# First loads of a UNet-like convolution kernel: image 0 cut into 6, 13 and 13 rows, the middle piece issued by ScalarE, and an 8-byte read of each row of the first weights

## The reference, cut to what matters

```python
def _gn(v, G=32, eps=1e-05):
    g = v.reshape(B_, G, C_ // G, H_, W_)
    m = jnp.mean(g, axis=(2, 3, 4), keepdims=True)
    s = jnp.var(g, axis=(2, 3, 4), keepdims=True)
    return ((g - m) / jnp.sqrt(s + eps)).reshape(v.shape)
...
    x = basic_block(x, e0b0c1, e0b0c2)       # 3x3 convs at 64x64
    x = basic_block(x, e0b1c1, e0b1c2)
    f0 = x
    x = basic_block(x, e1b0c1, e1b0c2, stride=2, ds=e1b0ds)   # 32x32
    x = basic_block(x, e1b1c1, e1b1c2)
    f1 = x
    x = basic_block(x, e2b0c1, e2b0c2, stride=2, ds=e2b0ds)   # 16x16
    x = basic_block(x, e2b1c1, e2b1c2)
    x = (relu(deconv2(x, dec0w) * BN_S) + f1) * BN_S
    x = (relu(deconv2(x, dec1w) * BN_S) + f0) * BN_S
...
    x = x + _L0_conv_ref(_gn(x), ...)
```

## Time and profile before

| | us |
|---|---|
| median of three timed runs | 92.99 |
| the profiled execution | 93.48 |
| its span, first to last instruction | 91.3 |
| PE busy | 83.4 (91% of the span) |
| DVE busy | 63.1 (69%) |
| ACT busy | 44.8 (49%) |
| POOL busy | 28.0 (31%) |

### The profile page before, as it was taken

The page is one execution under the profiler, slowest core; times in us unless marked ns, Lnnn a source line. Parts: engine busy times, 40 slices in busy tenths (PEclk is TensorE's granted clock), DMA queues, the critical chain, the costliest instruction groups (busy, mean ns, idle before and its releaser), DMA issues.

```text
span 91.3 us, 1542 instructions
## 1 busy us (share of the span) xinstructions
PE 83.4 (91%) x537; PEld 74.4 (81%) x537; DVE 63.1 (69%) x181; ACT 44.8 (49%) x94; POOL 28.0 (31%) x45
## 2 busy tenths in 40 slices
PE   5976999999999999999999999999999999998700
PEld 3764999998777799999977778999999999886500
DVE  5577999799858799556626479999368785343820
ACT  6006014778435066644513369899700399952300
POOL 7400060999920000743330001100990007000320
PEclk9999999999999999999999999999999999999955
DMA  2879810034681012640000000000000000000094
GB/s 31 251 215 321 288 71 0 7 115 125 149 268 63 2 43 83 215 119 6 0 0 0 0 4 0 0 0 0 7 0 0 0 0 4 7 0 0 14 327 118
DMA packets 4183, 6.51 MB, mean 71 GB/s; under 512 B 464, under 2 KB 2000, under 8 KB 4176
## 3 DMA queue, kind: packets, MB, share of 16 engines
q1 hardware_dynamic: 4176, 6.42, 23.0%
HBM read 5.37 MB, written 1.05 MB: 70 GB/s over the span
## 4 chain that ended last, share of the span: by engine, by line
PE 84%; DMA 6%; SPq 2%; ACT 2%; POOLq 1%; issue 1%; DVE 0%
PE psum L804 79%; DMA raw<-e0b0c_in 6%; PE psum L838 2%; PE psum L944 1%; SPq L412 1%; PE psum L1002 1%; POOLq L168 1%; ACT w_e0b0c L503 1%; PE psum L831 1%; SPq L416 0%; ACT shared L582 0%; ACT result L585 0%; DVE even L729 0%; PE psum L824 0%; POOLq L494 0%
## 5 line engine op out<-in xcount | busy, mean ns | idle before, releaser
L470 POOL TENSOR_TENSOR odd<-relu,odd 128x363 fp32r<-128x363 f32 x12 | 13.5, 1141 | 15.8 <-ACT odd L544 15.8
L804 PE MATMUL psum<-shared,w_e0b0c 128*128 128x364 f32 x72 | 12.5, 332 | 0.9 <-ACT w_e0b0c L503 0.9
L804 PEld LDWEIGHTS psum<-shared,w_e0b0c 128*128 128x128 f32 x72 | 11.9, 189 | 1.2 <-issue 1.1
L804 PE MATMUL psum<-shared,w_e0b1c 128*128 128x364 f32 x72 | 12.2, 329 | 0.0
L804 PEld LDWEIGHTS psum<-shared,w_e0b1c 128*128 128x128 f32 x72 | 12.1, 188 | 0.1
L804 PE MATMUL psum<-odd,w_e0b0c 128*128 128x512 f32 x48 | 11.9, 410 | 0.0
L804 PE MATMUL psum<-odd,w_e0b1c 128*128 128x512 f32 x48 | 11.9, 410 | 0.0
L720 DVE SCALAR_TENSOR_TENSOR relu<-psum,inside 128x363 f32<-128x363 f32 (+2 forms) x18 | 8.7, 491 | 3.7 <-PE psum L804 3.6
L804 PEld LDWEIGHTS psum<-odd,w_e0b1c 128*128 128x128 f32 x48 | 9.1, 190 | 2.5
L804 PEld LDWEIGHTS psum<-odd,w_e0b0c 128*128 128x128 f32 x48 | 9.1, 190 | 2.5
L544 ACT ACTIVATE odd<-relu 128x363 fp32r<-128x363 f32 x12 | 6.2, 519 | 7.4 <-DVE relu L720 7.4
(11 more groups left out here) (126 smaller groups left out, 140.4 us busy)
## 6 DMA issues: line engine op xcount, KB each, us to landing
out<-result SPq DMA_DIRECT2D x3, 256.0 KB, 3.1
x_sb<-x_in SPq DMA_DIRECT2D x4, 160.0 KB, 4.2
raw<-e0b0c_in SPq DMA_DIRECT2D x2, 256.0 KB, 5.3
raw<-e0b1c_in SPq DMA_DIRECT2D x2, 256.0 KB, 5.4
raw<-e1b1c_in SPq DMA_DIRECT2D x2, 256.0 KB, 2.9
raw<-e2b1c_in SPq DMA_DIRECT2D x2, 256.0 KB, 2.6
raw<-e1b0c_in SPq DMA_DIRECT2D x1, 448.0 KB, 3.7
raw<-e2b0c_in SPq DMA_DIRECT2D x1, 448.0 KB, 4.0
```

The source lines that it names most:

```text
L470: pool.tensor_tensor(split_of(piece, 1), fp32_of(piece), split_of(piece, 0).bitcast(F32), ALU.subtract).then_inc(lo_ready, 1)
L804: last = pe.matmul(target, w, moving, start=(first and n == 0), stop=(final and n == len(terms) - 1), skip_group_check=skip)
```

## The change

`STATS_ROWS` becomes 6, 13 and 13 rows, for both images. For image 0 SP leaves out the piece with number `BY_ACT_QUEUE` (rows 6 to 18), and ACT issues it as its first instruction. ACT then issues a second DMA, which reads the first two floats of each of the 128 rows of the weights e0b0c1 in HBM into a new tile `touched`, which nobody reads. SP waits for that DMA before the first store. Image 1 is still loaded by SP alone, in pieces of 6, 13 and 13 rows. `bn_stats` of image 0 runs on the pieces in the same order as before (rows 0 to 5, 6 to 18, 19 to 31).

```diff
-STATS_ROWS = [(0, 10), (10, 12), (22, 10)]
+STATS_ROWS = [(0, 6), (6, 13), (19, 13)]
+BY_ACT_QUEUE = 1
...
+        touched = sb("touched", [P, 2])
...
+        w_touched = sem("w_touched")
...
                 for n, (row, rows) in enumerate(STATS_ROWS):
+                    if image == 0 and n == BY_ACT_QUEUE:
+                        continue
                     sp.dma_start(x_sb[:, image, row:row + rows, :],
                                  x[:, image, row:row + rows, :]).then_inc(x_loaded[image][n], 16)
...
+            sp.wait_ge(w_touched, 16)
             stores = [(0, 1), (1, 1), (2, 2), (4, 2), (6, 2)]
...
+            row, rows = STATS_ROWS[BY_ACT_QUEUE]
+            act.dma_start(x_sb[:, 0, row:row + rows, :],
+                          x[:, 0, row:row + rows, :]).then_inc(x_loaded[0][BY_ACT_QUEUE], 16)
+            act.dma_start(touched[:], weights[0][:, 0, 0:2]).then_inc(w_touched, 16)
             act.wait_ge(ground_set, 1)
             act.activation(scratch[:, 0, 7:8], eps4[:, 0:1], ACT.Sqrt)
```

## The result

Six timed runs of the changed kernel have a median of 93.74 us (93.45 to 94.05), six of the kernel before 93.01 us (92.73 to 93.26). The ratio is 1.0059, with a 95% interval of 1.0034 to 1.0085: the change makes the kernel slower by about 0.55 us (0.73 us between the two medians). Forecast was 92.5, 0.5 us faster. The profiled executions hide most of this: 93.64 us after against 93.48 before, spans 91.5 and 91.3.

What follows compares the result with a forecast made beforehand. PE's start was taken as bound by the late first weights, landing at 7.80 us. PE's convolution 0.50 us earlier, low weights +0.03, all else 0: -0.47, rounded to -0.5, from 92.99 to 92.5 us; range 92.0 to 93.4.

Steps and rivals of the forecast that it cites:

- The weights' side: First weights' landing and ACT's rounding ahead of PE's first convolution: ready at 8.46 us, 0.50 us to give.
- the map's side: Statistics of x, spread and rounded rows 0 to 11 ahead of PE's first convolution: ready at 7.96 us.
- Steps 1 and 2: Weights issued earlier on SP (0.2 us), ACT's 8-byte read warming them: landing between 7.6 and 5.5 us, by 6.99 assumed.
- the second rival: The read warms nothing, only the issue is saved: gain 0 to 0.48 us, by value 0.2, 92.8 us; chance 0.20.
- Step 3: Image 0 cut to 6/13/13, middle piece by ACT: end of the statistics unmoved at 5.39 us, bounds 0.3 either side.
- Steps 4 to 6: ACT's issues ahead of its table load, SP's wait for `w_touched`, image 1 in 6, 13, 13: cost nothing.
- What is late next: PE start at 8.05 us by the map's side; low weights lose at most 0.05; image 1 keeps 0.8 us slack.
- the first rival: Two queues feed x faster, statistics end at 4.97, PE starts at 7.63: gain 0.9, 92.1 us; chance 0.14.
- The third: Slow first reads move ahead of x and delay its last piece: 0.7 us slower, 93.7 us, at most 1.6; chance 0.16.

Runs made afterwards that it cites:

- e2: The kernel before plus the 8-byte read alone, x in 10/12/10 all issued by SP: 0.9997 of the kernel before.
- e9: The kernel before with pieces of 10/11/11 rows, all issued by SP: 1.0019 of the kernel before.
- e6: The kernel before with pieces of 13/13/6 rows, all issued by SP: 0.9984 of the kernel before.
- e1: The kernel after without the 8-byte read, middle piece still issued by ScalarE: 1.0034 of the kernel before, median 93.56 us.
- e11: The kernel after without the 8-byte read, a second time: 1.0032 of the kernel before.
- e5: The kernel before with the middle piece of 10/12/10 rows issued by ScalarE, no read: 1.0010 of the kernel before.
- e3: The kernel before with pieces of 6/13/13 rows, all issued by SP, no read: 1.0038 of the kernel before, median 93.62 us.
- e15: The kernel before with pieces of 6/13/13 rows for both images, all issued by SP, a second time: 1.0077 of the kernel before.
- e16: The kernel before with 6/13/13 rows for image 0 alone, image 1 at 10/12/10, all issued by SP: 1.0062 of the kernel before.
- e4: The kernel before once more, no edit: 0.9990 of the kernel before, median 93.17 us, profiled execution 93.61 us.
- e8: The kernel after again, unchanged: 1.0058 of the kernel before.
- e7: The kernel before with pieces of 6/14/12 rows, all issued by SP: 1.0016 of the kernel before.
- e17: The kernel before with pieces of 6/16/10 rows, all issued by SP: 1.0005 of the kernel before.
- e12: The kernel after with four 8-byte reads of each row of the first weights in place of one: 1.0092 of the kernel before.
- e13: The kernel before with pieces of 13/13/6 rows, all issued by SP, a second time: 0.9987 of the kernel before.
- e14: The kernel before with pieces of 12/14/6 rows, all issued by SP, a second time: 1.0022 of the kernel before.

## Why the prediction was wrong

**What bounds the kernel: the reading of one profile.** The weights' side ahead of the map's side by 0.50 us was true of that execution and not of the kernel. Of the eighteen experiments only e2 has PE released by the weights' side at all, and there the map's side was ready with it (8.02 and 7.99 us). The landing at 7.8 us is the latest of all twenty profiles. A warning stood in the numbers: the profiled execution, 93.48 us, lay above all three timed runs, and near the top of the 92.8 to 93.6 of later ones. By the estimate above a timed median of 93.0 means a PE start near 8.1 us, which is just where the prediction wanted to bring it. So in a good part of the executions the forecast gain was there before the change; no profile of the unchanged kernel caught one of these, the nearest are e2 (8.14), e9 (8.03) and e6 (8.08).

**Steps 1 and 2, the early issue and the read.** The landing of the weights moved from 7.8 to 6.2 us, inside the range of 5.5 to 7.6. But e1 and e11 show it without the read, e5 without the cut, and e3, e15 and e16 (6.2 to 6.5 us) without read or second queue. So the second rival, the read warms nothing, was right about the read, and the reason that I gave for late weights, a first-read cost that a small read could pay, is not borne out by the runs. How much of the landing is the issue that was saved and how much the scatter between executions is open; the kernel before itself had 6.7 us in e4.

**Step 3, the cut.** This is the step that failed: the end of the statistics was taken as unmoved, and it moved by 0.6 us. The sum of the three `bn_stats` was right: 363 and 573 ns forecast, 358 and 578 measured in the kernel after:

```profile
L618 DVE BATCH_NORM_STATS2 stats<-x_sb 128x6 f32<-128x416 f32 x4 | 2.1, 578 | 0.0
L618 DVE BATCH_NORM_STATS2 stats<-x_sb 128x6 f32<-128x192 f32 x2 | 0.7, 358 | 1.2 <-DMA x_sb<-x_in 1.2
```

What was wrong is the end of the statistics, taken at 5.39 with bounds of 0.3 on either side; it came at 5.98 us, and at 5.87 in e8. Two terms were mis-sized, and in the kernel after each gives the delay by itself. The last landing was held at 4.84; it is 5.37 in the kernel after, which with the hand-over and 0.58 of `bn_stats` is 5.98, and 5.3 as a mean with 13 rows last. And the first piece landed at 4.53, past the bound of 0.27 later than 3.94; 0.09 of hand-over and 1.36 of back-to-back `bn_stats` are 5.98. In e8 the first piece is in at 4.08, within the bound, DVE idles 0.25 us ahead of the third piece, and the statistics still end at 5.87: the last landing is enough. The delay by the second queue was priced too low as well. Against equals, the first pieces of 6 rows, it is not 0.27 us but 0.7 to 1.7: they land at 2.9 to 3.4 us when SP issues all (e3, e7, e15, e16, e17) and at 4.1 to 4.6 beside ScalarE's load (after, e1, e8, e11, e12). Step 3 also took the end of the statistics before to hang "on the first piece's landing and on nothing else". The third `bn_stats` started at 5.39 - 0.48 = 4.91 us, only 0.07 behind the last landing, so there was next to nothing to give on that side.

**Steps 4 to 6** held. The table load moved to 1.64 us, ACT still waited 4.2 us behind it. SP's wait for the read cost nothing: the read had landed at 5.5 us, long before the stores. e16 against e15 shows no cost of image 1's pieces beyond their intervals.

**What is late next, and the sum.** From the end of the statistics to the rounded rows is 2.6 us again, 5.98 to 8.58; the step to PE is 0.14 and not 0.09 when DVE is the releaser. Every later slack held: 348 matmuls without a gap. So the path behind the statistics was read rightly and the two landings that feed it were not. One thing on it was left out, PE's matmuls on zeros ahead of the sum (e13 and e14 above). In the kernel before they end at 5.24 us and in e4 at 5.95, so the first rival's statistics at 4.97 would have met them in an execution like e4.

**The rivals.** The third, x is delayed and this makes it slower, has the right sign and the right place, the last piece and the statistics, with too small a chance (0.16); that its middle, 93.7 us, is the measured time is luck in part, since most of the delay has another cause. Its mechanism, stalls of the 8-byte read that are moved ahead of x, is a part at most: e8 and e12 against e11 give 0.14 to 0.25 us for a read, and e3, e15 and e16, with no read and one queue, lose as much as the kernel after. That e1 and e11, with the second queue and no read, lose only 0.3 us may mean that the second queue gives back a little of what the cut costs and the read takes it again; the intervals allow it and don't show it. The larger part, the long last piece, I had seen in step 3 as "each has to be there in time" and then priced at nothing. The rule of the Trainium skill that was weighed there, that issuing from a second engine saves only the issue (DMA: Bandwidth & Descriptors, Issuing engines are not separate DMA queues), agrees with the time of e5, the second queue alone: 1.0010 (0.9995 to 1.0024). What changed there is the order of the landings, the first piece later and the weights earlier.

None of the versions tried beats the kernel before clearly. The best, 13/13/6, is 0.13 to 0.16% faster in two runs, with intervals that end at 1.0000 and 1.0007.

## What to carry to other kernels

Compare the profiled execution's own time with the timed runs before using its chain: if it lies above them all, the wait that it shows may be that execution's alone, and a second profile of the same kernel is the cheapest experiment. Where a chain goes through "last byte landed, then process the last piece", don't make the last piece longer: the cut with 13 rows last in place of 10 cost 0.35 to 0.7 us here. Making it shorter gained at most 0.15 us (13/13/6) and lost 0.2 in another cut (12/14/6), because then the first landing set the end of the statistics, and in three of the four profiles PE's own filler work cost time behind it. An early first piece is worth nothing if the processor then idles for the next one. Work that only fills an engine's idle time stands on the path too, when what it waits for comes early. Two sides that join at one instruction should both be given their spread over executions, not one value each.

## What the runs showed of the hardware

- The landing of the same 160 KB load, issued at the same 1.64 us behind the same two loads, was 3.2 us behind its issue in one execution and 3.6 in the next, that of the first weights 5.2 and 4.1.
- A load of 1 KB in 128 rows of 8 bytes, queued behind 208 KB of x on ScalarE's queue, took 4.4 us to land, as long as 256 KB did (4.1); as the first load of that queue, in e2, it took 2.9.
- Four such reads on the second queue, 4 KB in all, made the kernel 0.56 us slower by the ratios, 0.38 by the medians (e12 against e11).
- A first load of 96 KB landed 2.2 to 2.7 us behind its issue in five profiles with all loads on one queue, and 3.3 to 3.9 in five with a load of 208 KB issued at the same time on the other.
- 22 matmuls on zeros, the same in every kernel, took from 3.9 (e17) to 4.9 us (e14) at a granted clock of 1.00 in the profile's windows.
- With the loads of x on two queues 4.5 to 8 us moved data at 304 to 346 GB/s in six profiles; with all on one queue at 219 to 299. In e5 the kernel's time did not show it.
